# Sixteen stack loads move from bursts on SyncE's queue to ScalarE's queue, two behind each of eight steps

## What is computed

```python
x = _ln(src) * (1.0 + scale) + shift                      # scale, shift from the timestep
q, k, v = x @ Wq + bq, x @ Wk + bk, x @ Wv + bv           # 16 heads of 16 features
scores = einsum('bhqd,bhkd->bhqk', q / 4, k) + attention_bias   # 8 x 16 x 512 x 512
scores = where(src_mask, -inf, scores)
ctx = einsum('bhqk,bhkd->bhqd', softmax(scores), v)
x = x + (ctx @ Wo + bo)
x = x + _gelu2((_ln(x) * g2 + beta2) @ W1 + b1) @ W2 + b2
```

## Time and profile before

| | us |
|---|---|
| median of 3 runs | 1203.0 (1199.84 to 1203.21) |
| profiled execution | 1203.06 |
| its span in the trace | 1201.2 |
| busy in the span: PE / DVE / ACT / POOL | 1045.7 / 818.0 / 782.1 / 350.5 |

### The profile page before, as it was taken

The page is one execution under the profiler, slowest core; times in us unless marked ns, Lnnn a source line. Parts: engine busy times, 40 slices in busy tenths (PEclk is TensorE's granted clock), DMA queues, the critical chain, the costliest instruction groups (busy, mean ns, idle before and its releaser), DMA issues. The chain is left out here.

```text
span 1201.2 us, 22037 instructions
## 1 busy us (share of the span) xinstructions
PE 1045.7 (87%) x6042; PEld 671.9 (56%) x6128; DVE 818.0 (68%) x2056; ACT 782.1 (65%) x1238; POOL 350.5 (29%) x464
## 2 busy tenths in 40 slices
PE   2689999989989989989998999797599998998863
PEld 2446556546645545645664655354477776776641
DVE  5666776776757658667686767474655787977665
ACT  2367887877768768767786778574446657666432
POOL 0205115113212211511411231000565357545421
PEclk9889999999989989999998999899699999999966
DMA  6576996987995895797598688853101101111001
GB/s 226 175 235 206 311 262 207 317 211 236 263 275 177 234 315 194 213 314 222 192 307 226 217 245 229 260 192 106 53 36 35 35 19 52 35 35 36 18 18 35
DMA packets 148585, 209.41 MB, mean 174 GB/s; under 512 B 19104, under 2 KB 79392, under 8 KB 148512
## 3 DMA queue, kind: packets, MB, share of 16 engines
q1 hardware_dynamic: 148512, 208.63, 57.9%
HBM read 187.62 MB, written 20.97 MB: 174 GB/s over the span
## 5 line engine op out<-in xcount | busy, mean ns | idle before, releaser
L690 DVE CUSTOM_DVE_ANT_0 prob<-s_bank,big 128x512 f32<-128x512 f32 x512 | 346.1, 687 | 190.9 <-PE s_bank L549 133.4
L835 ACT ACTIVATE prob<-prob,nmax 128x512 f32<-128x512 f32 x512 | 363.6, 723 | 86.7 <-DVE nmax L690 82.3
L558 PEld LDWEIGHTS t_bank<-ident,prob 128*128 128x128 f32 x2048 | 241.5, 142 | 214.2 <-issue 83.7
L558 PE MATMUL t_bank<-ident,prob 128*128 128x128 f32 x2048 | 322.4, 281 | 11.0 <-ACT prob L835 4.6
L842 ACT COPY pt<-t_bank 128x512 f32<-128x512 f32 x320 | 184.7, 577 | 99.2 <-PE t_bank L558 96.6
L548 PE MATMUL s_bank<-stack_k,stack_q 128*128 128x512 bf16 x426 | 165.6, 389 | 32.2 <-DVE nmax L690 32.2
L549 PE MATMUL s_bank<-mterm_early,ident_bf 128*128 128x512 bf16 x448 | 173.8, 388 | 8.3 <-DMA stack_k<-pieces_dram 4.0
L699 DVE COPY pt<-t_bank 128x512 f32<-128x512 f32 x192 | 132.1, 688 | 41.3 <-PE t_bank L558 41.3
L571 PE MATMUL o_bank<-pt,val 128*32 128x512 f32 x1024 | 142.7, 633 | 0.7 <-ACT pt L842 0.7
L954 POOL TENSOR_SCALAR val<-vst 128x64 f32<-128x64 f32 x128 | 26.9, 243 | 296.8 <-PE o_bank L571 260.5
L1639 POOL TENSOR_TENSOR gl<-big,gh 128x512 fp32r<-128x512 f32 x64 | 87.2, 1371 | 86.8 <-DVE gh L1344 86.8
(11 more groups left out here) (176 smaller groups left out, 1623.5 us busy)
## 6 DMA issues: line engine op xcount, KB each, us to landing
big<-in_fside_Bx16xSxS SPq DMA_DIRECT2D x128, 1024.0 KB, 7.1
stack_q<-pieces_dram SPq DMA_DIRECT2D x128, 128.0 KB, 5.6
stack_k<-pieces_dram SPq DMA_DIRECT2D x128, 128.0 KB, 5.5
pieces_dram<-pieces SPq DMA_DIRECT2D x32, 384.0 KB, 7.1
xin<-in_x SPq DMA_DIRECT2D x8, 512.0 KB, 7.5
x_dram<-x SPq DMA_DIRECT2D x8, 512.0 KB, 3.1
big<-x_dram SPq DMA_DIRECT2D x8, 512.0 KB, 3.4
x1r<-x_dram SPq DMA_DIRECT2D x8, 512.0 KB, 4.4
```

The lines of the kernel that those rows point to most:

```text
L558: last = pe.transpose(t_bank[n % 2][:, c * P:(c + 1) * P], prob[:, n % NT, c * P:(c + 1) * P], ident[:])
L690: dve.tensor_tensor_reduce(out=prob[:, n % NT, :], in0=s_bank[n % 3][:, :], in1=bias[:, h % NB, t, :], scale=-1.0, scalar=3e38, op0=ALU.ad ...
L835: act.activation(tile, tile, ACT.Exp, bias=nmax[:, n % NT:n % NT + 1], scale=-1.0).then_inc(exped.sem, 1)
```

## The change

The stack loads of all samples but the first leave SP's program and stand in ScalarE's. `STACKS_FROM = (42, 4)` gives the first iteration for each half: for half 0 of the next sample iterations 42 to 49 of this one, for half 1 iterations 4 to 11 of the next sample itself. In each of these iterations, behind the exponential and the copy, ScalarE issues two transfers: the i-th of `stack_q` and the i-th of `stack_k`. In the first of the eight it waits for the scores that free the half and for the two stores of the pieces. The loads for the first sample stay on SP. The transfers, their sizes and their sources are unchanged.

```diff
-HEADS_OF_LOADS = dict(x1=2, expert=4, mask=5, store_0=7, store_1=11, stack_0=9)
+HEADS_OF_LOADS = dict(x1=2, expert=4, mask=5, store_0=7, store_1=11)
+STACKS_FROM = (42, 4)
...
-            def load_stack(b, c, first=False):
-                if not first:
-
-                    sp.wait_ge(scored.sem, scored.at(b, STEPS // 2 * (c + 1)))
-                    apart(sp, sp_apart)
+            def load_first_stack(c):
                 for qk, (stack, piece) in enumerate(((stack_q, QPIECE), (stack_k, KPIECE))):
-                    sp.wait_ge(pieces_out[c][qk].sem, pieces_out[c][qk].at(b, 16))
-                    apart(sp, sp_apart)
+                    sp.wait_ge(pieces_out[c][qk].sem, pieces_out[c][qk].at(-1, 16))
...
-                    if h == HEADS_OF_LOADS["stack_0"] and not last:
-                        load_stack(b, 0)
-                if not last:
-                    load_stack(b, 1)
...
+            def load_stack(b, c, i):
+                if i == 0:
+
+                    act.wait_ge(scored.sem, scored.at(b, STEPS // 2 * (c + 1)))
+                for qk, (stack, piece) in enumerate(((stack_q, QPIECE), (stack_k, KPIECE))):
+                    if i == 0:
+                        act.wait_ge(pieces_out[c][qk].sem, pieces_out[c][qk].at(b, 16))
+                    src = pieces_dram[:, qk, c, piece[i]].rearrange("(h e) t -> e h t", e=HD)
+                    act.dma_start(stack[i::NP8, c * HC:(c + 1) * HC], src).then_inc(stack_in[c].sem, 16)
...
+                    if not last and 0 <= n - STACKS_FROM[0] < NP8:
+                        load_stack(b, 0, n - STACKS_FROM[0])
+                    if not first and 0 <= n - STACKS_FROM[1] < NP8:
+                        load_stack(b - 1, 1, n - STACKS_FROM[1])
```

More of the change, by code:

```diff
@@ L495, in iteration @@
                         store_pieces(b, 1)
-                    if h == HEADS_OF_LOADS["stack_0"] and not last:
-                        load_stack(b, 0)
-                if not last:
-                    load_stack(b, 1)
             for c in range(DC):
                 store_pieces(-1, c, first=True)
-                load_stack(-1, c, first=True)
+                load_first_stack(c)
                 if c == 0:
```

## The result

Slower, by the predicted amount, and in part by luck. The median is 1215.7 us (4 runs, 1215.0 to 1217.6) against 1202.6 us for the kernel before on the same chip (4 runs, 1199.8 to 1203.2); the ratio is 1.0122, interval 1.0101 to 1.0143. The forecast was 1217 us. The profiled execution took 1216.13 us with a span of 1214.3, 13.1 us more than before. The sum was right, but three of its four terms were not, and their errors cancelled. That only shows stage by stage.

The account below looks back on a forecast made before the run. TensorE was taken as busiest (87% of the span), with TensorE, VectorE and ScalarE all full in iterations 42 to 49. Sum: 1203.06 + 38.5 - 15 - 10 = 1216.6, 1217 us; forecast's own range 1198 to 1232, wider range 1175 to 1260.

Parts of the forecast that it names:

- fast steps: Iterations 42 to 49, all three engines full: two issues a step stretch 7.6 us to 12.7, net 4.5 us per sample, seven times.
- slow steps: Iterations 4 to 11, with weighing and context work: 12.7 in place of 11.9 us, forecast 1 us per sample, seven times.
- jump: VectorE's 6 us stall where the loop jumps back: removing the burst gives 3 us each, five times, -15 us; bounds 0 and -37.
- last sample: VectorE's 9.40 us wait for a bias load behind SP's burst and small weight loads goes: -10 us, once.
- Rival 1: An issue costs ScalarE next to nothing: 1178 us; chance 14%.
- rival 3: On ScalarE, issue and arithmetic exclude each other: 1203 + 160 - 25 = 1338 us; chance 9%.
- rival 4: TensorE's clock falls in the stretched steps, some 7 us at half speed per sample: 24 us more, 1240 us; chance 14%.
- rival 2: Full relief where samples meet: VectorE's stall shrinks, TensorE doesn't pause, clock stays 1.00; -37 in place of -15, 1194 us; chance 12%.
- full overlap: Assumption for ScalarE's steps with issues: arithmetic already handed over runs while the next instruction issues.
- no way to regain it in the weighing steps behind: Behind iterations 42 to 49: TensorE, the sample's busiest engine, can't regain the lost time in the weighing steps.

Follow-up runs that it names:

- SP's burst behind head 1: Kernel before, with SP issuing half 1's burst behind head 1's bias load of the next sample, not at the sample's end; ScalarE issues none: 1186.7 us, ratio 0.9888.
- half 1 alone on ScalarE: Changed kernel, with half 0 put back as a burst on SP behind head 9; only half 1 issued by ScalarE: 1200.8 us, ratio 1.0000 to the kernel before.
- half 0 alone: Changed kernel, with half 1 put back as a burst on SP at the sample's end; only half 0 issued by ScalarE: 1208.8 us, ratio 1.0076 to the kernel before.

## Why the prediction was right, term by term

**The mechanism was right, the closeness of the sum was luck.** The four terms missed by -16.4 us (fast steps), +6.5 (slow steps), +10.9 (jump) and +0.1 (last sample), and the start, which the sum left out, took 1.7 us away. Together that is nearly nothing. ScalarE's issues take what SP's took, arithmetic runs beside them, the next exponential waits for them, and the eight fastest steps of the sample can't carry two each. TensorE and VectorE then wait, the data is in time, and the clock holds in the stretched steps. Rival 1 fell with the issue time of 0.54 to 0.62 us, rival 3, whose 160 us are 7 x (12.7 + 10.2), with the step of 1.34 us (issues and arithmetic one after the other would need 1.16 + 0.72 + 0.57 = 2.45), rival 4 with the clock of 1.00, rival 2 with the stall of 5.58 us. The "full overlap" of the prediction holds where the copy is ready. Where the copy waits, the issues stand behind it, as the prediction said in the same paragraph and then didn't use.

**The fast eight steps, 4.5 us forecast: 3.1 us in place and 2.2 net.** The prediction had 1.28 us for two issues and 0.3 us of small work taken from SP's bias loads. On ScalarE a step takes 1.34 us, of which 1.16 are the two issues, so the small work is under 0.2. Both parts were 0.12 us too large in each step; that is the mis-sized term. The "no way to regain it in the weighing steps behind" was wrong too: 51 to 57 gave back 0.9 us per sample. A likely reason is that copies and weighing left over from the fast steps are done sooner when these are slow; no run separates it, and with four issues per step nothing came back.

**The slow eight steps, 1 us forecast: 1.9 us.** In the inner samples over half of it, 1.0 of 1.7 us, comes in the first of them, from 2.45 to 3.42 us in the mean. There the prediction had the issues hidden. But the copy waits for its transpose, the issues come only behind it and the next exponential only behind them:

```profile
458.97 0.59 ACT L834 COPY pt<-t_bank 128x512 f32<-128x512 f32 x1 [1.64 <-PE t_bank L550]
459.14 0.54 ACTq L860 DMA_DIRECT2D stack_q<-pieces_dram  x1
459.72 0.61 ACTq L860 DMA_DIRECT2D stack_k<-pieces_dram  x1
460.45 0.72 ACT L827 ACTIVATE prob<-prob,nmax 128x512 f32<-128x512 f32 x1 [0.89 <-DVE nmax L682]
```

The view names VectorE for the last wait, but the rows that this exponential needs from VectorE were ready at 457.85 us. In all seven samples it starts within 0.12 us of the end of the second issue and 1.4 to 1.5 us behind the copy's start. In the kernel before that distance is 0.5 us, with one issue per step 0.9 at most. Of the other steps, short steps are stretched (0.79 to 1.32 us) and one long step gives back 0.4.

**The jump, 3 us each forecast: 0.8 us.** This step failed. I saw the stall fall into the burst and gave half a reason to the traffic. That it is a fetch was right, by its packet. But the burst changes the packet by only 0.3 us, and the length of the stall is mostly elsewhere: stalls are 4.7 to 6.5 us long at a share of 1.10 to 1.12, and 4.9 to 6.0 at 0.56 to 0.73. The written-out loop shows that the jump costs 5.2 us of the sample, nearly the 5.6 us for which VectorE stands in the kernel after. What sets the time ahead of the packet is open. It holds 0.5 of the 0.9 us by which the stalls are shorter with SP's burst behind head 1. The 3.4 us that the jump's bound and the last sample's term take for the clock were an estimate, half of some 7 us at half clock, and no run shows them by themselves. What the traces show is how long the granted clock is 0.50: in the kernel before 6.8 us at four of the five jumps and 3.4 at one (538.1 to 544.9 us in the sample of the earlier trace rows), after the change 6.8 at two and 3.4 at three; at the late bias load of the last sample it is 10.2 us before (756.6 to 766.8 us), and after the change there is no such stretch.

**The last sample, -10 us forecast: -10.7 us** (28.3 to 17.6 us in 13 to 25). The one wait for data in the earlier trace rows was worth its full length. The kernel with half 1 alone on ScalarE shows the same 10.7, and with SP's burst behind head 1 it is 8.4.

The terms with their measured sizes: +15.1 + 13.5 - 4.1 - 9.9 - 1.7 for the start = +12.9, against +13.1 in the span.

## What to carry to other kernels

An engine with arithmetic can issue transfers for nothing as long as each issue fits under what has been handed over already: here, in steps of 0.95 us full of arithmetic, one issue of 0.6 us was free, two cost 0.4 us a step and four 1.7. Before you move issues, look for the steps where the engine is full and for what the old place made late, since here the profit lay in one late bias load (8 to 11 us) and in the stretch behind the jump (4 to 8 us), and moving SP's burst gave both. And a stall of "issue" at a loop's jump isn't to be put down to the traffic beside it until a run without that traffic has been seen: writing the loop out on the one engine that stalls was worth 25 to 30 us, and the best of the other changes gave 17 us under the kernel before.

## What the runs showed of the hardware

- ScalarE can stall at its own jump too. With half 1 alone on ScalarE its first exponential behind each of the five jumps is late by 4.7 to 5.1 us, while in the kernels before, after and with half 0 alone it isn't:

```profile
543.46 0.72 ACT L840 ACTIVATE prob<-prob,nmax 128x512 f32<-128x512 f32 x1 [5.03 <-issue]
```

  In the trace's own numbering of ScalarE's instructions the loop runs from 188 to 452 there, from 205 to 468 with half 0 alone, from 188 to 434 before and from 205 to 486 after. So neither its length nor its first instruction decides alone. VectorE's loop has 374 instructions from jump to jump and stalled in every kernel that had it (55 stalls of 4.7 to 6.5 us in eleven kernels). No run shows what tells ScalarE's four loops apart.
- A fetch of instructions can be seen in the DMA view, as one packet of the queue "instruction" in each stall: 0.3 to 0.4 us long without the burst, 0.6 to 0.8 beside it. Where ScalarE stalls as well (half 1 alone), each stall has two. VectorE goes on 2.0 to 2.2 us behind the packet's end.
- An issue on ScalarE reached 1.4 to 1.8 us at times, the maxima of its rows above; on SP a bias load's reached 2.05 us. The median is not the whole price of an issue.
